# Folding the key projection of an attention layer into its query projection, with the order of the pipeline written anew

## What is computed

```python
def _L1_attn_ref(x, W, b):
    qkv = jnp.einsum('btc,cd->btd', x, W) + b
    q, k, v = jnp.split(qkv, 3, axis=-1)
    weights = jnp.einsum('btc,bTc->btT', q, k) * scale
    logits = jnp.where(mask == 0, jnp.float32(-9000000000000000.0), weights)
    attention = jax.nn.softmax(logits, axis=-1)
    return jnp.einsum('btT,bTc->btc', attention, v)
```

## Time and profile before

| | us |
|---|---|
| median of three runs (706.18 to 711.22) | 707.75 |
| the profiled execution | 708.59 |
| its span, from the first to the last instruction | 706.8 |
| PE busy | 662.7 |
| DVE busy | 585.6 |
| ACT busy | 479.4 |
| POOL busy | 310.7 |

### The profile page before, as it was taken

One profiled execution on the slowest core, in us unless ns is written; L12 is line 12 of the kernel. 1 busy time (PEld: TensorE's weight loads), 2 busy tenths in 40 slices (PEclk: granted clock), 3 DMA queues, 4 the chain that ended last, 5 costly groups with the idle time before them and its releaser, 6 DMA issues.

```text
span 706.8 us, 11728 instructions
## 1 busy us (share of the span) xinstructions
PE 662.7 (94%) x3654; PEld 510.9 (72%) x3654; DVE 585.6 (83%) x1873; ACT 479.4 (68%) x974; POOL 310.7 (44%) x793
## 2 busy tenths in 40 slices
PE   3778789999999999999999999999999999999994
PEld 2566677777868787777868787787868787766652
DVE  1566798889898998889898988889898988977772
ACT  2245476686877868786877868786877868666542
POOL 1336443345354535345354535445454535431311
PEclk9778899999999999999999999999999999999997
DMA  7000000001010000101010000101000000000001
GB/s 231 15 2 17 0 16 1 16 0 31 1 31 1 15 16 1 32 1 31 0 32 1 16 16 1 31 2 31 2 29 2 16 1 1 15 16 1 1 16 30
DMA packets 18686, 12.69 MB, mean 18 GB/s; under 512 B 704, under 2 KB 18240, under 8 KB 18368
## 3 DMA queue, kind: packets, MB, share of 16 engines
q1 hardware_dynamic: 18624, 11.95, 5.6%
HBM read 7.75 MB, written 4.19 MB: 17 GB/s over the span
## 4 chain that ended last, share of the span: by engine, by line
PE 88%; ACT 4%; DVE 3%; POOL 2%; issue 1%; DMA 1%; SPq 0%; ACTq 0%; DVEq 0%; POOLq 0%
PE bank L552 17%; PE bank L346 11%; PE bank L348 10%; PE bank L347 10%; PE bank L355 10%; PE bank L462 2%; PE bank L435 2%; PE bank L406 2%; PE bank L479 2%; PE bank L425 2%; PE bank L473 2%; PE bank L474 2%; PE bank L450 2%; PE bank L519 2%; PE bank L500 1%; PE bank L506 1%
## 5 line engine op out<-in xcount | busy, mean ns | idle before, releaser
L552 PE MATMUL bank<-hid,whole 128*128 128x512 f32 x288 | 146.8, 594 | 0.3 <-DVE hid L1360 0.3
L346 PE MATMUL bank<-x3T_hi,w_hi 128*128 128x512 f32 x288 | 138.1, 480 | 0.1
L903 ACT ACTIVATE silu<-bank 128x512 f32<-128x512 f32 x144 | 86.3, 599 | 75.8 <-PE bank L348 72.9
L1350 DVE TENSOR_TENSOR gu<-silu,bank 128x512 f32<-128x512 f32 x128 | 86.7, 677 | 32.6 <-ACT silu L903 17.8
L348 PE MATMUL bank<-x3T_hi,w_lo 128*128 128x512 f32 x288 | 113.6, 394 | 0.0
L1632 POOL TENSOR_TENSOR moment<-stats 128x4 f32<-128x4 f32 x192 | 46.5, 274 | 151.9 <-DVE stats L1164 124.6
L347 PE MATMUL bank<-x3T_lo,w_hi 128*128 128x512 f32 x288 | 112.7, 391 | 0.0
L1360 DVE TENSOR_TENSOR hid<-gu,bank 128x512 f32<-128x512 f32 x128 | 87.3, 682 | 3.2 <-PE bank L552 1.8
L346 PEld LDWEIGHTS bank<-x3T_hi,w_hi 128*128 128x128 f32 x288 | 54.2, 188 | 28.7 <-issue 9.6
L1618 POOL TENSOR_TENSOR qk<-rope_c,rope_s 128x512 f32<-128x512 f32 x32 | 40.6, 1277 | 75.4 <-DVE rope_s L1126 75.4
L1632 POOL TENSOR_TENSOR rstd<-moment,whole 128x4 f32<-128x4 f32 x64 | 64.8, 1012 | 5.0
(11 more groups left out here) (196 smaller groups left out, 1643.6 us busy)
## 6 DMA issues: line engine op xcount, KB each, us to landing
x_in<-x SPq DMA_DIRECT2D x16, 256.0 KB, 2.8
out<-x SPq DMA_DIRECT2D x16, 256.0 KB, 2.3
whole<-w_whole SPq DMA_DIRECT2D x1, 1198.5 KB, 5.6
w_raw<-w SPq DMA_DIRECT2D x1, 1152.0 KB
w_raw<-w SPq DMA_DIRECT2D x1, 546.0 KB, 6.9
whole<-w_whole SPq DMA_DIRECT2D x16, 32.0 KB
whole<-w_whole SPq DMA_DIRECT2D x1, 64.0 KB
```

What stands on the lines that cost most here:

```text
L346: mm(out, wh, mh, start=True, stop=False)
L552: mm(YB[:], whole[:, a:a + P], hid[:, c % 2], start=c == 0, stop=c == CHUNKS).then_inc(p_w2.sem, 1)
L903: fn(silu[:, c % 2], GB[:], ACT.Silu).then_inc(a_silu.sem, 1)
L1350: tt(gu[:, c % 2], silu[:, c % 2], UB[:], ALU.mult).then_inc(v_gu.sem, 1)
```

## The change

With biases bq and bk, the logit of rows t and T is (x_t Wq + bq) times (x_T Wk + bk). Multiplied out, the part that varies with both rows is x_t M x_T with M = Wq Wk^T; a part that depends on t alone drops out of the softmax, and two parts are left: x_T times Wk bq, which goes with x_T (it is added as a bias to x_t M), and a scalar per row. The changed kernel makes M and the bias vectors once on the chip (`fold_keys` on PE and ACT, `fold_bias` on DVE). Each block then has one product, x M, instead of two, and the scores take the transposed block itself as keys. The remaining scalar per row is made as a 129th column of the value product and its bias; since the masked logits of a row all carry it, it enters through the exponent's bias, which POOL forms in `c_shift` from the row maximum that DVE takes without negation.

Beside that, `c_value` is cut into two halves of two tiles, one into B0 ahead of the query product and one into B1 behind it, on PE and on DVE; ACT's `c_norm` gets a wait for the last reader of its buffer; `split_late` moves in the first turns, on ACT ahead of `a_vT_(1)`, on DVE from ahead of `c_value(0)` to behind `a_kv(2)`; and the orders of `first_turns`, `turn` and `last_turns` are written anew on PE, ACT, DVE and POOL. SP's list is the same.

```diff
+            def fold_keys():                                   # PE
+                nc.tensor.transpose(B0[:, 0:P], raw("cq"), ident)
+                nc.tensor.transpose(B0[:, P:2 * P], raw("ck"), ident).then_inc(p_fold.sem, 1)
+                pe.wait_ge(a_fold.sem, 1)
+                pe.wait_ge(v_fold.sem, 3)
+                wqT, wkT = foldT[:, 0:P], foldT[:, P:2 * P]
+                mm(B1[:, 0:P], wqT, wkT, start=True, stop=True)
+                mm(B1[:, P:P + 1], wkT, const("bcq"), start=True, stop=True)
+                mm(B1[:, P + 1:P + 2], wqT, const("bck"), start=True, stop=True)
+                mm(B1[:, P + 2:P + 3], const("ones"), b_qk[:], start=True, stop=True).then_inc(p_fold.sem, 1)
...
             def c_project(n):
+                if not started(n):
+                    pe.wait_ge(a_fold.sem, 5)
                 pe.wait_ge(a_xT[2].sem, a_xT[2].at(n))
-                mm(B1[:], raw("cq"), xT[2][:], start=True, stop=True).then_inc(p_cq.sem, 1)
-                mm(B0[:], raw("ck"), xT[2][:], start=True, stop=True).then_inc(p_ck.sem, 1)
-
-            def c_value(n):
-                pe.wait_ge(a_cq.sem, a_cq.at(n))
-                for t in range(TILES):
-                    last = mm(tile(B1, t), tile(xT[2], t), raw("cv"), start=True, stop=True)
+                mm(B1[:], m_qk[:], xT[2][:], start=True, stop=True).then_inc(p_cq.sem, 1)
+
+            def c_value(n, half):
+                pe.wait_ge(a_xT[2].sem, a_xT[2].at(n))
+                if half == 1:
+                    pe.wait_ge(a_cq.sem, a_cq.at(n))
+                b = B1 if half else B0
+                for i in range(2):
+                    last = mm(b[:, i * SEQ:i * SEQ + CVW], tile(xT[2], 2 * half + i), w_cv[:], start=True, stop=True)
                 last.then_inc(p_cv.sem, 1)
 
             def c_scores(n):
-                pe.wait_ge(a_ck.sem, a_ck.at(n))
                 for s, b in ((0, B0), (1, B1)):
-                    if s == 1:
-                        pe.wait_ge(v_cv.sem, v_cv.at(n))
+                    pe.wait_ge(v_cv.sem, v_cv.at(n, s + 1))
...
-                    k0, k1 = tile(ckT, 2 * s), tile(ckT, 2 * s + 1)
+                    k0, k1 = tile(xT[2], 2 * s), tile(xT[2], 2 * s + 1)
...
+            def fold_keys():                                   # ACT
+                act.wait_ge(p_fold.sem, 1)
+                fn(foldT[:], B0[:, 0:2 * P], ACT.Copy).then_inc(a_fold.sem, 1)
+                act.wait_ge(p_fold.sem, 2)
+                fn(m_qk[:], B1[:, 0:P], ACT.Copy, scale=C_SCALE).then_inc(a_fold.sem, 1)
...
-            def c_qkv(n):
+            def c_query(n):
...
-                fn(cqT[:], B1[:], ACT.Identity, scale=C_SCALE, bias=bcq_s[:]).then_inc(a_cq.sem, 1)
-                act.wait_ge(p_ck.sem, p_ck.at(n))
-                fn(ckT[:], B0[:], ACT.Identity, bias=const("bck")).then_inc(a_ck.sem, 1)
+                fn(cqT[:], B1[:], ACT.Identity, bias=r_b[:]).then_inc(a_cq.sem, 1)
 
             def c_exp(n):
                 for s, b in ((0, B0), (1, B1)):
-                    act.wait_ge(v_max.sem, v_max.at(n, 2 * s + 2))
+                    act.wait_ge(g_max.sem, g_max.at(n, 2 * s + 2))
...
             def c_norm(n, odd):
                 act.wait_ge(g_ln[2].sem, g_ln[2].at(n))
+                if n_is(n, 2):
+                    act.wait_ge(v_res[3].sem, v_res[3].at(n - 2))
...
+            def c_shift(n):                                    # POOL
+                for s in range(SEQS):
+                    pair, row = slice(2 * s, 2 * s + 2), cv[:, 2 * s:2 * s + 2, P]
+                    pool.wait_ge(v_max.sem, v_max.at(n, 2 * s + 2))
+                    pool.wait_ge(v_cv.sem, v_cv.at(n, s + 1))
+                    tt(top_l[:, pair], top_s[:, pair], row, ALU.add).then_inc(g_max.sem, 1)
+                    pool.wait_ge(g_max.sem, g_max.at(n, 2 * s + 1))
+                    tt(neg_max[:, pair], row, top_l[:, pair], ALU.subtract).then_inc(g_max.sem, 1)
```

More of the change, by code:

```diff
@@ L46 @@
 KV = P + HEADS
+CVW = P + 1
 LOGITS = PROJ + len(RANKS)
@@ L104, in second, with first_turn @@
     return isinstance(i, int) and i == 1
+def first_turn(i):
+    return isinstance(i, int) and i == 0
 def started(n):
@@ L176, in build @@
         b_logit = sb("b_logit", [P, LOGITS])
-        bcq_s = sb("bcq_s", [P, 1])
+        foldT = sb("foldT", [P, 2 * P])
+        m_qk = sb("m_qk", [P, P])
+        r_b = sb("r_b", [P, 1])
+        b_qk = sb("b_qk", [P, 1])
+        w_cv = sb("w_cv", [P, CVW])
+        b_cv = sb("b_cv", [P, CVW])
         x_in = sb("x_in", [P, 2, TILES, P])
@@ L505, in c_av @@
                 for s in range(SEQS):
-                    mm(tile(B1, 2 * s), probT[:, s, 0:P], cv[:, 2 * s], start=True, stop=True)
-                    mm(tile(B1, 2 * s + 1), probT[:, s, P:2 * P], cv[:, 2 * s], start=True, stop=False)
-                    last = mm(tile(B1, 2 * s + 1), probT[:, s, 2 * P:3 * P], cv[:, 2 * s + 1], start=False, stop=True)
+                    mm(tile(B1, 2 * s), probT[:, s, 0:P], cv[:, 2 * s, 0:P], start=True, stop=True)
+                    mm(tile(B1, 2 * s + 1), probT[:, s, P:2 * P], cv[:, 2 * s, 0:P], start=True, stop=False)
+                    last = mm(tile(B1, 2 * s + 1), probT[:, s, 2 * P:3 * P], cv[:, 2 * s + 1, 0:P], start=False, stop=True)
                 last.then_inc(p_av.sem, 1)
@@ L627, in first_turns @@
                 a_xT_(2, 0, 1)
+                c_xT(0)
                 a_out(1)
-                c_xT(0)
+                c_value(0, 0)
+                c_project(0)
                 a_vT_(2)
-                c_project(0)
-                c_value(0)
+                c_value(0, 1)
                 c_scores(0)
@@ L786, in _ @@
             fn(escale[:], clamp_t[:], ACT.Exp).then_inc(setup_a.sem, 1)
-            fn(bcq_s[:], const("bcq"), ACT.Copy, scale=C_SCALE).then_inc(setup_a.sem, 1)
             fn(up_x[:], const("up", 3 * SUB), ACT.Copy).then_inc(setup_a.sem, 1)
@@ L910, in turn @@
                 a, b, c, d, e = live(i), live(i - 1), live(i - 2), live(i - 3), live(i - 4)
+                if a: x0_hi(i)
                 if d: d_silu(i - 3, 0)
-                if a: x0_hi(i)
-                if second(i): split_late()
                 if c: c_exp(i - 2)
@@ L1292, in c_max, with c_value @@
                     for i, (a, w) in enumerate(((0, P), (P, 2 * P))):
-                        red(neg_max[:, 2 * s + i:2 * s + i + 1], b[:, a:a + w], AX.X, ALU.max, negate=True).then_inc(v_max.sem, 1)
-            def c_value(n):
-                dve.wait_ge(p_cv.sem, p_cv.at(n))
-                tt(cv[:], tiles(B1[:]), const("bcv").unsqueeze(1).broadcast_to([P, TILES, P]), ALU.add).then_inc(v_cv.sem, 1)
+                        red(top_s[:, 2 * s + i:2 * s + i + 1], b[:, a:a + w], AX.X, ALU.max).then_inc(v_max.sem, 1)
+            def c_value(n, half):
+                if not started(n):
+                    dve.wait_ge(a_fold.sem, 5)
+                dve.wait_ge(p_cv.sem, p_cv.at(n, half + 1))
+                tt(cv[:, 2 * half:2 * half + 2], by_tile(B1 if half else B0)[:, :, 0:CVW],
+                   b_cv[:].unsqueeze(1).broadcast_to([P, 2, CVW]), ALU.add).then_inc(v_cv.sem, 1)
             def c_res(n):
@@ L1378, in turn @@
                 if d: d_gu(i - 3, 1)
-                if b: b_norm(i - 1, 0)
                 if d: d_hid(i - 3, 1)
                 if d: d_gu(i - 3, 2)
+                if b: b_norm(i - 1, 0)
                 if b: b_norm(i - 1, 1)
                 if d: d_hid(i - 3, 2)
+                if a: conv_tap(i, 1)
                 if d: d_gu(i - 3, 3)
+                if a: a_kv(i)
                 if b: b_logits(i - 1)
-                if a: a_kv(i)
+                if second(i): split_late()
+                if a: conv_tap(i, 2)
@@ L1407, in turn @@
-                if second(i): split_late()
-                if c: r_groups(i - 2, 3)
                 if d: d_gu(i - 3, 7)
                 if d: d_hid(i - 3, 7)
+                if c: r_groups(i - 2, 3)
                 if c: r_groups(i - 2, 4)
+                if a: a_res(i, odd)
                 if d: d_gu(i - 3, 8)
-                if a: a_res(i, odd)
+                if b: c_value(i - 1, 0)
                 if c: r_combine(i - 2)
-                if b: c_value(i - 1)
+                if b: c_value(i - 1, 1)
```

409 lines of the change are left out of this document (219 added, 190 removed).

## The result

The changed kernel takes 703.34 us (median of 13 runs, 700.15 to 705.71), the kernel before 707.81 in as many: a ratio of 0.9932, 95% interval 0.9915 to 0.9948. That is 4.5 us, of 16 forecast; the time lies 3.3 above the forecast range. Faster it is, but by less than 1%.

The account below looks back on a forecast made before the run. PE work was taken to bound twelve steady turns and latencies the two ends: 708.6 - 10.2 - 3.6 - 2.4 = 692.4, or 691.6 against the median, taken as 692 us; range 686 to 700.

Parts of the forecast that it names:

- the -6.0 for the ends: First and last turns together: 6.0 us gained, -3.6 in the first turns and -2.4 in the last.
- Last turns, -2.4: Last turns: one key product goes, -0.86, and block 14's routing is ready earlier; -2.4 us in all, ends -4 and +1.
- The shift: Four POOL additions before ACT's exponentials: 0.6 us per pair of maxima, bounds 0.4 and 1.3, covered on PE by 0.17 us.
- First turns, -3.6: First turns: key products -2.6, fold +1, new order -2; -3.6 us in all, ends -7 and +3.
- a first steady turn at 133 or later: Sign in the changed profile: this start, instead of near 129, makes the term of the ends wrong.
- Steady turns, -10.2: Twelve steady turns: 0.85 us less each, 10.2 us gained; 3 to 9 if the hand-offs fail.
- the walk: New PE order of a steady turn followed with old durations: it closes at 38.94 us, with margins of 0.1 to 0.2.
- The third rival: Slower: POOL's shift costs much more than 0.6 us and ACT keeps vT's copies behind the exponentials; priced at 720, chance 0.04.
- Value product: Value product on PE: 129 columns instead of 128 in each of four parts, 0.007 us more.
- table loads: ACT in a steady turn: two exponentials back to back save two table loads of 1.28 us each.
- POOL against DVE: Shared SBUF interfaces: a collision moved or added each turn would take back up to 11 us; the sum has none.
- The first (ends give nothing, 698 to 699): Rival on the ends: fold at the low clock in block 0's chain, +3, reordering gains 0; 698 to 699, chance 0.2.

## Why the prediction was wrong

*What bounds the kernel.* Right: three accounts, PE's work in the turns and latencies at the ends. The sum then did not hold to it, and this is the step that failed: the -6.0 for the ends. It counted the four key products there as PE work (-2.6 and -0.86), where PE was not the limit, and gave 3.5 to the new order. Measured is +2.6 (+1.75 and +0.8), and -1.5 with the waits filled (-2.4 and +0.9). The kernel without the product shows 0.00 for three of the four and 0.03 for the other, in the old order. "As long as the operands of that work are ready" was the right condition, and what was not ready was the bank that ACT's copy of the queries had yet to free: the product removed had been its cover.

*Last turns, -2.4.* The new order fills that place again (block 15, from the query product to the scores: 2.61 with a down product in it; before, to the next chunk, 2.72 without one), but the last stretch then waits elsewhere (PE of the changed kernel, transposes of block 14's probabilities; before, the second of them waited 0.34):

```profile
609.71 0.55 PE L527 MATMUL bank<-whole,prob 128*128 128x128 f32 x3 [0.68 <-ACT prob L911]
610.51 0.55 PE L527 MATMUL bank<-whole,prob 128*128 128x128 f32 x3 [0.26 <-ACT prob L911]
```

The shift stands ahead of these exponentials, and the chunk that stood between the transposes and the products before now stands behind them. The shift is not all of it. Without it (new orders) the first of these waits is gone, but PE waits for DVE's x behind them, 0.73 in place of 0.18:

```profile
607.83 0.55 PE L527 MATMUL bank<-whole,prob 128*128 128x128 f32 x3 [0.26 <-ACT prob L911]
609.10 0.66 PE L368 MATMUL bank<-whole,x 128*128 128x128 f32 x4 [0.73 <-DVE x L1222]
```

So the last turns cost 0.8 to 0.9 where -2.4 (ends -4 and +1) was forecast. Their new order is worth 0.4 (97.1, and 97.5 with the old last turns), not 1.5. What else makes them longer than before stays open.

*First turns, -3.6.* With the waits filled it is -2.4, inside the bounds; without, +1.75 in one pair of executions. By the forecast's own sign, a first steady turn at 133 or later, the term of the ends was wrong. What the sum left out is that this stretch hangs on the clock granted behind PE's idle time, and that this differs between executions of one list: the start varies from 129.8 to 134.7. The low clock was named only as a price for the fold's ten instructions; what these cost by themselves no run isolates. That the new order keeps the clock low for longer than the old one is not shown: the 0.80 of before lies within the 0.53 to 0.81 of the new list.

*Steady turns, -10.2.* The mechanism was right, the size not: -7.6. PE has no wait in the new order, as the walk said, but the walk used the old lengths. 0.12 of the missing 0.23 a turn is the new addresses. The other 0.1 is spread over pieces whose lengths changed with their neighbours, up and down; no experiment took it back, and it stays open. That the kernel without the product also comes to 39.17 has another cause, its waits for the copy of the queries and for `comb`.

*The shift.* Right: 0.58 a pair against 0.6, covered in the steady turn. The third rival named the right mechanism, and the old steady order, which lacks the cover, shows its price at that: 0.5 a turn. *Value product, table loads, the wait of c_norm, POOL against DVE:* as forecast; DVE's busy time did not grow, so the collision of the earlier trace rows took nothing in a turn (the DVE operation there usually takes 0.22, not 0.28), and the Trainium skill's rule on the shared SBUF interfaces ("GPSIMD Engine Reference", section 8) has no case here.

*Rivals.* The first (ends give nothing, 698 to 699) was nearest in kind, but still had the three products of the first turns in it and 0.85 a turn. With 0.63 a turn and nothing for the products its sum would be 707.75 - 7.6 + 3 to 4 = 703 to 704, the time measured. That is in part luck: its +3 was the fold's own price, which no run shows.

## What to carry to other kernels

An instruction that is taken off the busiest engine gives its time back only where that engine is the limit, and there only if it was not the cover of a handover behind it: before counting it, look at what the next instruction on that engine waits for. Lengths taken from the old trace hold only in the old neighbourhood and at the old addresses. Where an engine's clock follows its activity, the time of a ramp differs between executions of one order, so compare such changes with the waits filled before judging the order, and see whether each filling still ends before its wait does.

## What the runs showed of the hardware

- TensorE's time for the same products depends on where its operands lie in SBUF: with the buffers 704 to 2,656 bytes higher, the nine chunks of a turn took 14.22 us, at the old addresses 14.11.
- A piece between the same starts differs by up to 0.17 us with its neighbours (the numerator: 1.010 behind the gate, 0.840 behind a product of 512 columns), and what it gains the next one can lose.
- Idle time of 4.15 us on TensorE was followed by 1.2 GHz for the nine microseconds from 78 to 87 in the changed kernel's profile. The Trainium skill ("TensorE: Matmul & The Clock Gate", "HAM oscillation — how this bites in real kernels") tells of idle gaps after which work runs at the low clock; the trace agrees. How long it lasts differs between executions: over the nine microseconds behind that idle time, with the same list, the clock was 0.53, 0.58, 0.80 and 0.81 in four.
- Useless products in TensorE's waits were worth 5 us to one kernel (703.34 to 698.38). The same filling moved the kernel before by 0.17%, which its interval doesn't tell from nothing.
